# VectorE's tables behind the last pair's low halves, and part of the bias and group 0's projections ahead of the last bias rows

## The chip, the cores and the metric

The kernel runs on one core of a Trainium2 chip. The metric is device microseconds (us) of one execution; lower is better. TensorE (PE in the profile), VectorE (DVE), ScalarE (ACT), GpSimd (POOL) and SyncE (SP, which issues all the DMAs here) have a queue of instructions each, taken in order, and meet only at semaphores.

## The reference

The input `x` has the shape (1, 160, 160, 64). With all the rest left out, what is computed is:

```python
z = ln_c(x)                                          # layer norm over the 64 channels
bias = einsum('bijd,dh->bhij', z, Wb)                # 4 heads, from ALL 160 rows of z
q, k, v = z @ Wq, z @ Wk, z @ Wv                     # per row r: 160 tokens, 4 heads of 32
sim = einsum('brihe,brjhe->brhij', q, k) * scale + bias[:, None]
sim = where(mask, sim, -1e9)
o = softmax(sim) @ v
x = x + (o * sigmoid(z @ Wg)) @ Wo
t = ln_t(x)
probs = softmax(t @ router_w + router_b); top 2 of 8, normed
x = x + sum of the two experts' (t @ expert_w + expert_b), weighted
```

The bias of every attention row is made from all 160 rows of `z`, so nothing after `sim` can start until the layer norm of the whole input is done.

## The kernel before

**Phase 1** runs over 20 pairs of groups (a group is 4 rows of 160 tokens, a pair 8 rows) with `run_phase1`. Of pair n, VectorE makes sums and centres the input, ScalarE squares it, GpSimd scales it, ScalarE takes the float16 high half (`high`, L494) and VectorE the low half (`low`, L680, tile `hl`). TensorE turns it (`turn`, L975), ScalarE copies the turned pair out (`make_xs`, L502, semaphore `xs_made`), TensorE multiplies it by `Wb` (`bias_of`, L987), ScalarE evacuates that (L513, semaphore `b_evac`), and SyncE writes the turned pair to `xs_all` (L239) and the bias rows to a scratch in HBM (L245). The work on one pair is spread over the steps n to n+3. The high and low halves exist because every product is made of float16 pairs.

**Between the phases** VectorE makes tables: `small_tables` (ones and folds), `mask_tables` (the mask as floats, `pen`, `some`, the `pick` matrices), `weight_halves` (high and low halves of all weights, then semaphore `w_ready`), `expert_bias_halves`. All of this is called inside `phase1` at step n == PAIRS (20), which in program order is ahead of the low halves of the last pair, pair 19. Each of these instructions waits for the one before it (`prep`). SyncE reads the bias back in another layout: rows 0 to 127 (the main part) with one DMA into the borrowed tile `pt_a` (L320, semaphore `b_loaded[0]`), and, after the last pair's rows are written, rows 128 to 159 with eight DMAs into `bias_s` and `bias_q` (L326, L328, `b_loaded[1]`). `bias_tables` (VectorE, L758 to L781) and `turn_bias` (TensorE, L1008 to L1014) make of both the tiles `bm` (i along the partitions) and `bt_hi`, `bt_lo` (j along the partitions), with hand-written semaphores `b_step` and `b_turned`; at its end VectorE raises `b_ready`.

**Phase 2** runs over 40 groups with `run_steps`; a step n works on up to seven groups at once. TensorE waits for `w_ready` and, after `turn_bias`, for `b_ready`. Its first work is then `project_qk` of group 0 (L1032, four pieces: q and k, each in two halves of columns), each followed by `qk_high` on ScalarE (L523) and `qk_low` on VectorE (L792); then `max_scores` of group 0 (L1043 adds the bias into `psS`, L1048 and L1053 the products), `row_max` on VectorE (L800), `turn_max`, `scores` (L1068 the bias, L1075 the products) and so on. All orders are written out by hand. A PSUM bank is handed on by `take`, which makes TensorE wait for the last reader of the bank.

Of the kernel before, what the change touches and what calls it, by code (L numbers as in the profile page):

```python
# [5 lines left out]
ALU = mybir.AluOpType  # L6
# [5 lines left out]
P = 128  # L12
# [31 lines left out]
def build(nc, x, Wq, Wk, Wv, Wg, Wo, Wb, router_w, router_b, expert_w, expert_b, mask, out):  # L44
    with ExitStack() as ctx:
# [15 lines left out]
        turned16 = [[banks16[3], banks16[1]], [psS[:, k, :].bitcast(F16) for k in range(2)]]  # L61
        ps_bias = [ps_o, ps_r]

        ident = sb("ident", [P, P])
# [152 lines left out]
        def on(g):  # L217

            return not isinstance(g, int) or 0 <= g < GROUPS

        N_WLOAD = 2 * 6 + 2 + T + 3 * T
# [262 lines left out]
        def _(act):  # L484
# [127 lines left out]
            def step(n, a):  # L612
                b = 1 - a
                if on(n + 1): qk_high(n + 1, b, 0, 1, ps_x)
# [6 lines left out]
                if on(n + 2): qk_high(n + 2, a, 1, 0, ps_m)  # L621
                if on(n + 2): qk_high(n + 2, a, 0, 0, ps_x)
# [8 lines left out]
                if on(n + 2): qk_high(n + 2, a, 1, 1, ps_o)  # L631
# [8 lines left out]
        def _(dve):  # L640
# [54 lines left out]

            def mask_tables():
# [4 lines left out]
                prep(dve.tensor_scalar(pen[:], pen[:], some[:], None, ALU.mult))  # L701
                for c in range(2):
                    prep(dve.tensor_scalar(pick[c][:], pen[:, 0:P], fold[:, 3:4], fold[:, c:c + 1], ALU.mult, ALU.add))
# [11 lines left out]

            def weight_halves():
                prep(dve.tensor_scalar(w_raw[:, Q0:K0], w_raw[:, Q0:K0], SCALE, None, ALU.mult))
                prep(dve.tensor_scalar(w_raw[:, K0:WALL], w_raw[:, K0:WALL], some[:], None, ALU.mult))
                for part in (slice(Q0, WALL), slice(V0, B0), slice(O0, Q0)):
# [14 lines left out]
            def phase1(n, a, do):  # L734
# [18 lines left out]
            def bias_tables():  # L753

                b32 = bias32[:].rearrange("p h s j -> p (h s j)")[:, 0:H * N].rearrange("p (h j) -> p h j", h=H)
                over_heads = lambda v: v.unsqueeze(1).broadcast_to([P, H, N])
                dve.wait_ge(b_loaded[0], 16)
                prep(dve.tensor_tensor(b32, b32, over_heads(mask_f[:]), ALU.mult))  # L758
                prep(dve.tensor_copy(bias_c[:], b32[:, :, P:N]))
                dve.nop().then_inc(b_step, 1)  # L760
                prep(dve.tensor_tensor(bm3[:, :, 0:2, :], b32.unsqueeze(2).broadcast_to([P, H, 2, N]),
                                       pen[:].unsqueeze(1).unsqueeze(1).broadcast_to([P, H, 2, N]), ALU.add))
                dve.wait_ge(b_loaded[1], 16 * 2 * H)
                prep(dve.tensor_tensor(bias_s[:], bias_s[:], mask_f[:], ALU.mult))
                dve.nop().then_inc(b_step, 1)
                prep(dve.transpose(bias_t[:, P:N], bias_s[:, P:N]))
                prep(dve.tensor_tensor(bias_q[:], bias_q[:], over_heads(mask_f[:]), ALU.mult))
                prep(dve.tensor_tensor(bm3[:, :, 2, :], bias_q[:], over_heads(pen[:]), ALU.add))
                dve.wait_ge(b_turned, 2)
                i_rest = ps_o[:, 0:P].rearrange("j (h i) -> j h i", h=H)  # L770
                prep(dve.tensor_copy(bias_t[:, 0:P], ps_r[:, 0:P]))
                prep(dve.tensor_copy(bt3_hi[:, :, 0, 0:P], psS[:, :, 0:P]))
                prep(dve.tensor_copy(bt3_hi[:, :, 0, P:N], i_rest))
                prep(dve.tensor_tensor(bt3_lo[:, :, 0, 0:P], psS[:, :, 0:P], bt3_hi[:, :, 0, 0:P], ALU.subtract))
                prep(dve.tensor_tensor(bt3_lo[:, :, 0, P:N], i_rest, bt3_hi[:, :, 0, P:N], ALU.subtract))
                dve.nop().then_inc(b_step, 1)
                prep(dve.tensor_copy(bt3_hi[:, :, 1, :], bt3_hi[:, :, 0, :]))
                prep(dve.tensor_copy(bt3_lo[:, :, 1, :], bt3_lo[:, :, 0, :]))
                dve.wait_ge(b_turned, 3)
                prep(dve.tensor_copy(bt3_hi[:, :, 2, :], psS[:, :, 0:N]))  # L780
                prep(dve.tensor_tensor(bt3_lo[:, :, 2, :], psS[:, :, 0:N], bt3_hi[:, :, 2, :], ALU.subtract))  # L781
                dve.nop().then_inc(b_ready, 1)

            bias_tables()

            def qk_low(g, a, k, c, bank):

                dve.wait_ge(qkh_done[k][c], g + 1)
                for half_ in range(2):
                    need(dve, sa_done[half_], g - 1)  # L790
                cols = slice(CH * c, CH * c + CH)
                dve.scalar_tensor_tensor(out=qk_lo[a][k][:, cols], in0=bank[:, 0:CH], scalar=1.0 / UP,  # L792
                                         in1=qk_hi[a][k][:, cols], op0=ALU.mult, op1=ALU.subtract).then_inc(qkl_done[k][c], 1)

            def row_max(g, c):
# [131 lines left out]
            def step(n, a):  # L927
# [10 lines left out]
                if on(n - 3): weigh(n - 3, 4, ps_o)  # L938
                if on(n + 2): qk_low(n + 2, a, 1, 0, ps_m)
                if on(n + 2): qk_low(n + 2, a, 0, 0, ps_x)  # L940
                if on(n + 1): row_max(n + 1, 1)
# [8 lines left out]
                for k in range(10, 13):  # L950
                    if on(n - 2): route(n - 2, k)
                if on(n + 2): qk_low(n + 2, a, 1, 1, ps_o)
                for k in range(1, 3):
# [6 lines left out]
                if on(n - 1): mean2(n - 1, b)  # L960
                if on(n + 2): qk_low(n + 2, a, 0, 1, ps_x)
                if on(n + 2): row_max(n + 2, 0)
# [7 lines left out]
        def _(pe):  # L970
# [246 lines left out]
            def step(n, a):  # L1217
# [9 lines left out]
                if on(n - 2): project_out(n - 2, ps_m)  # L1227
                if on(n + 1): project_qk(n + 1, b, 0, 1, ps_x)
                if on(n - 1): project_v_rest(n - 1, b, ps_o)
# [12 lines left out]
                if on(n - 3): experts(n - 3, b, 4, ps_o)  # L1242
                if on(n + 2): project_qk(n + 2, a, 1, 0, ps_m)
                if on(n + 2): project_qk(n + 2, a, 0, 0, ps_x)
                if on(n - 2): turn2(n - 2, a, ps_r, banks16[2])
# [5 lines left out]
                if on(n): row_sums(n, a, ps_m)  # L1251
                if on(n + 2): project_qk(n + 2, a, 1, 1, ps_o)
# [33 lines left out]
```

## Time and profile before

| | us |
|---|---|
| median of 3 runs | 954.86 |
| lowest and highest | 951.77 and 955.25 |
| time of the profiled execution | 954.15 |
| its span, first to last instruction | 952.3 |

The page's own time of 954.15 us and the span of 952.3 us differ by 1.85 us, which lie before the first and behind the last instruction. Phase 1 ends near 98 us in the trace, the stretch between the phases reaches to about 131 us, and phase 2 takes the remaining 820 us. In the rows, "busy" is time in an instruction, "idle before" is the wait ahead of it on its engine, and what stands behind "<-" is the instruction that ended that wait.

### The profile page before, as it was taken

How to read it: one execution, taken by the hardware profiler on the slowest of the kernel's cores; microseconds unless marked ns; L12 is line 12 of the kernel's file. 1: busy time of each engine (PE TensorE's matmuls, PEld its weight loads, DVE VectorE, ACT ScalarE, POOL GpSimd, SP SyncE). 2: the span in 40 equal slices, each digit the busy share in tenths (PEclk: the TensorE clock that was granted, in tenths of full speed). 3: DMA queues.
4: the chain of work that ended last, by engine and by line, in shares of the span. 5: the costliest groups of instructions: out<-in, count | busy, mean ns of one | idle time of the engine just before them, and what ended most of it. 6: DMA issues, size and time to landing. Idle time of an engine off the chain costs nothing.

```text
span 952.3 us, 40372 instructions
## 1 busy us (share of the span) xinstructions
PE 791.2 (83%) x15174; PEld 500.7 (53%) x15174; DVE 767.4 (81%) x1808; ACT 487.8 (51%) x1061; POOL 663.4 (70%) x1092
## 2 busy tenths in 40 slices
PE   1444147999999999999999999999999999999753
PEld 1333123666665666666656665666566656565521
DVE  7776553588889888988898889888888888888764
ACT  3777113465555554655465546554655465546411
POOL 7899000257777767777777777767776777677877
PEclk9999998999999999999999999999999999999965
DMA  3554310000110011001100110011001100100000
GB/s 115 181 194 166 101 39 23 24 23 31 51 38 30 28 48 34 28 28 48 34 28 28 47 36 28 28 48 34 28 28 41 41 28 28 46 32 24 17 13 17
DMA packets 38088, 44.76 MB, mean 47 GB/s; under 512 B 6416, under 2 KB 32656, under 8 KB 38032
## 3 DMA queue, kind: packets, MB, share of 16 engines
q1 hardware_dynamic: 38032, 43.99, 13.9%
q8 instruction: 38, 0.62, 0.3%
q14 instruction: 18, 0.15, 0.0%
HBM read 14.48 MB, written 9.83 MB: 26 GB/s over the span
## 4 chain that ended last, share of the span: by engine, by line
PE 34%; DVE 34%; issue 20%; POOL 8%; ACT 1%; DVEq 1%; DMA 1%; SPq 0%; POOLq 0%; ACTq 0%
DVE negm L800 6%; PE psS L1068 6%; DVE rinv L816 4%; PE psS L1043 4%; POOL ln_s L393 4%; DVE prod L915 3%; PE ps_o L1125 3%; PE ps_x L1125 2%; PE ps_x L1128 2%; PE ps_o L1128 2%; DVE og L831 2%; DVE rt L877 2%; DVE q_lo L792 2%; POOL xn L396 2%; DVE ogu L823 1%
## 5 line engine op out<-in xcount | busy, mean ns | idle before, releaser
L443 POOL TENSOR_TENSOR add<-prod 128x256 f32<-128x256 f32 x160 | 116.3, 727 | 100.7 <-DVE prod L915 100.7
L800 DVE TENSOR_REDUCE negm<-psS 128x12 f16<-128x1920 f32 x80 | 146.0, 1825 | 12.0 <-PE psS L1053 8.2
L494 ACT ACTIVATE hl<-xn 128x320 f16<-128x320 f32 (+1 forms) x60 | 33.5, 559 | 158.3 <-POOL xn L396 156.8
L393 POOL TENSOR_TENSOR ln_s<-ln_v,half 128x5 f32<-128x5 f32 (+1 forms) x60 | 97.0, 1616 | 4.7
L448 POOL TENSOR_TENSOR add<-add 128x128 f32<-128x128 f32 x200 | 91.0, 455 | 0.1
L425 POOL TENSOR_TENSOR rinv_lo<-rinv,rinv_hi 128x160 f16<-128x160 f32 x40 | 19.7, 492 | 100.9 <-ACT rinv_hi L564 100.9
L533 ACT ACTIVATE pt_b<-psS 128x1920 f32<-128x1920 f32 x40 | 70.8, 1771 | 19.6 <-PE psS L1087 15.6
L450 POOL TENSOR_TENSOR ymix<-add 128x64 f32<-128x64 f32 x200 | 64.3, 322 | 15.7
L489 ACT ACTIVATE sq<-xc 128x320 f32<-128x320 f32 (+1 forms) x60 | 33.3, 556 | 81.7 <-POOL xc L409 73.1
L431 POOL TENSOR_TENSOR og_lo<-og,og_hi 128x320 f16<-128x320 f32 x80 | 61.6, 791 | 17.3 <-ACT og_hi L570 17.3
L1043 PE MATMUL psS<-bm,ident 128*128 128x480 f16 (+1 forms) x320 | 68.4, 337 | 5.9 <-ACT pt_a L533 3.3
L1068 PE MATMUL psS<-bt_hi,ident 128*128 128x320 f16 (+1 forms) x320 | 67.9, 335 | 2.3 <-DVE negm L800 2.3
L831 DVE TENSOR_TENSOR og<-ogu,ps_x 128x320 f32<-128x320 f32 x40 | 19.5, 488 | 62.0 <-issue 59.1
L1068 PE MATMUL psS<-bt_lo,ident 128*128 128x320 f16 (+1 forms) x320 | 68.0, 336 | 0.0
L540 ACT ACTIVATE v_main<-ps_x 128x512 f32<-128x512 f32 x40 | 23.9, 597 | 66.3 <-PE ps_x L1139 66.3
L396 POOL TENSOR_TENSOR xn<-xc,ln_s 128x320 f32<-128x320 f32 (+1 forms) x60 | 54.0, 901 | 5.3 <-POOL ln_s L393 1.1
L915 DVE SCALAR_TENSOR_TENSOR prod<-ps_m,coef 128x512 f32<-128x512 f32 x80 | 54.8, 684 | 2.5 <-PE ps_m L1201 2.5
L1191 PE MATMUL ps_m<-w_hi,og_hi 128*128 128x64 f16 x200 | 27.9, 207 | 30.7 <-DVE rinv L816 22.9
L533 ACT ACTIVATE pt_a<-psS 128x1280 f32<-128x1280 f32 x40 | 49.5, 1237 | 2.3 <-PE psS L1077 2.3
L816 DVE RECIPROCAL rinv<-ps_m 128x160 f32<-128x160 f32 x40 | 45.8, 1145 | 1.7 <-PE ps_m L1101 1.7
L1043 PEld LDWEIGHTS psS<-bm,ident 128*128 128x128 f16 x320 | 27.2, 98 | 35.4 <-ACT pt_a L533 16.6
L1191 PEld LDWEIGHTS ps_m<-w_hi,og_hi 128*128 128x128 f16 x200 | 23.9, 128 | 38.0 <-DVE rinv L816 19.2
(263 smaller groups left out, 2819.3 us busy)
## 6 DMA issues: line engine op xcount, KB each, us to landing
xin<-in_x SPq DMA_DIRECT2D x20, 320.0 KB, 2.9
xs_all<-xs_pair SPq DMA_DIRECT2D x20, 320.0 KB, 2.5
xs_q<-xs_all SPq DMA_DIRECT2D x40, 160.0 KB, 2.1
xs_v<-xs_all SPq DMA_DIRECT2D x40, 160.0 KB, 2.1
xin<-in_x SPq DMA_DIRECT2D x40, 160.0 KB, 2.2
out<-res SPq DMA_DIRECT2D x40, 160.0 KB, 1.9
bias_scratch<-b_stage SPq DMA_DIRECT2D x20, 160.0 KB, 2.4
pt_a<-bias_scratch SPq DMA_DIRECT2D x1, 320.0 KB, 3.2
```

The costliest lines, as they stand in the source:

```text
L393: pool.tensor_tensor(ln_s[a][:, 3, 0:w], ln_v[a][:, 0:w], half[:, 0:w], ALU.pow).then_inc(own, 1)
L396: pool.tensor_tensor(xn[a][:, 0:w], xc[a][:, 0:w], ln_s[a][:, 3, 0:w].unsqueeze(2).broadcast_to([P, w, D]), ALU.mult).then_inc(own, 1)
L431: pool.tensor_tensor(og_lo[:, cols], og[:, cols], og_hi[:, cols], ALU.subtract).then_inc(ogl_done[c], 1)
L443: pool.tensor_tensor(add1[t % 2][:], prod_of(t)[:, 0:4, :], prod_of(t)[:, 4:8, :], ALU.add).then_inc(mix_step[t], 1)
L448: pool.tensor_tensor(add2[t % 2][:], add1[t % 2][:, 0:2, :], add1[t % 2][:, 2:4, :], ALU.add).then_inc(mix_step[t], 1)
L450: pool.tensor_tensor(ymix[:, t, :], add2[t % 2][:, 0, :], add2[t % 2][:, 1, :], ALU.add).then_inc(mix_step[t], 1)
L533: act.activation(pt[:].rearrange("p h s i -> p h (s i)"), psS[:, :, 0:slots * N], ACT.Exp).then_inc(exp_done[c], 1)
L800: dve.tensor_reduce(negm[c][:, :, 0:slots], psS[:, :, 0:slots * N].rearrange("i h (s j) -> i h s j", s=slots), AX.X, ALU.max, negate=True) ...
L816: dve.reciprocal(rinv[:], bank[:, 0:N]).then_inc(rinv_done, 1)
L915: dve.scalar_tensor_tensor(out=prod_of(t)[:], in0=bank[:].rearrange("p (e c) -> p e c", e=E), scalar=1.0 / UP, in1=coef[:, t, :].unsqueeze ...
L1043: mm(psS[:, h, 0:(3 - c) * N], lhsT=ident16[:], rhs=bm3[:, h].rearrange("i s j -> i (s j)")[:, 0:(3 - c) * N], start=True, stop=False)
L1068: mm(psS[:, h, 0:slots * N], lhsT=ident16[:], rhs=part[:, h].rearrange("j s i -> j (s i)")[:, 0:slots * N], start=part is bt3_hi, stop=False)
```

## The change

Five edits are made together.

1. The tables are no longer made inside `phase1`. All of phase 1 comes first on VectorE, the low halves of pair 19 among it.
2. The tables are cut in parts: `key_mask` (mask, `pen`, `some`, and the scaling of the q and k weights) and the halves of the output, q and k weights (`slice(Q0, WALL)` is q and k) come first and raise `w_ready` to 1; then come `small_tables` and `mask_tables`.
3. The projections of group 0 are issued ahead of `turn_bias` on TensorE, with their high halves on ScalarE and their low halves on VectorE behind `mask_tables`. They use the banks `ps_x` and `ps_m`, each twice. In the steps, `later(g)` leaves them out for group 0.
4. `bias_tables` is cut in two. `bias_of_keys` does what rows 0 to 127 allow, and the halves of the other weights and of the expert bias come behind it; `w_ready` becomes 2 there. `bias_of_rest` waits for the last rows.
5. The copies of slot 0 into slot 1 of `bt_hi` and `bt_lo` are cut in two: the first 128 columns are copied as before, and the last 32 are made a second time from PSUM.

```diff
@@ phase 1 of VectorE, step n == PAIRS
-                if not do[0]:
-                    if n == PAIRS:
-                        dve.wait_ge(w_loaded, 16 * N_WLOAD)
-                        small_tables()
-                        mask_tables()
-                        weight_halves()
-                        expert_bias_halves()
@@ VectorE, behind run_phase1
-            bias_tables()
+            dve.wait_ge(w_loaded, 16 * N_WLOAD)
+            key_mask()
+            weight_halves([slice(Q0, WALL)])
+            small_tables()
+            mask_tables()
+            for c in range(2):
+                for k in range(2):
+                    qk_low(0, 0, k, c, ahead_bank[k])
+            def bias_of_keys():
...
+                dve.wait_ge(b_loaded[0], 16)
+                prep(dve.tensor_tensor(b32, b32, over_heads(mask_f[:]), ALU.mult))
+                prep(dve.tensor_copy(bias_c[:], b32[:, :, P:N]))
+                dve.nop().then_inc(b_step, 1)
+                prep(dve.tensor_tensor(bm3[:, :, 0:2, :], twice(b32),
+                                       pen[:].unsqueeze(1).unsqueeze(1).broadcast_to([P, H, 2, N]), ALU.add))
+                dve.wait_ge(b_turned, 1)
+                prep(dve.tensor_copy(bias_t[:, 0:P], ps_r[:, 0:P]))
+                prep(dve.tensor_copy(bt3_hi[:, :, 0, 0:P], psS[:, :, 0:P]))
+                prep(dve.tensor_tensor(bt3_lo[:, :, 0, 0:P], psS[:, :, 0:P], bt3_hi[:, :, 0, 0:P], ALU.subtract))
+                prep(dve.tensor_copy(bt3_hi[:, :, 1, 0:P], bt3_hi[:, :, 0, 0:P]))
+                prep(dve.tensor_copy(bt3_lo[:, :, 1, 0:P], bt3_lo[:, :, 0, 0:P]))
+            def bias_of_rest():
...
+                dve.wait_ge(b_loaded[1], 16 * 2 * H)
+                prep(dve.tensor_tensor(bias_s[:], bias_s[:], mask_f[:], ALU.mult))
+                dve.nop().then_inc(b_step, 1)
+                prep(dve.transpose(bias_t[:, P:N], bias_s[:, P:N]))
+                dve.nop().then_inc(b_step, 1)
+                prep(dve.tensor_tensor(bias_q[:], bias_q[:], over_heads(mask_f[:]), ALU.mult))
+                prep(dve.tensor_tensor(bm3[:, :, 2, :], bias_q[:], over_heads(pen[:]), ALU.add))
+                dve.wait_ge(b_turned, 2)
+                i_rest = ps_o[:, 0:P].rearrange("j (h i) -> j h i", h=H)
+                for s in range(2):
+                    prep(dve.tensor_copy(bt3_hi[:, :, s, P:N], i_rest))
+                    prep(dve.tensor_tensor(bt3_lo[:, :, s, P:N], i_rest, bt3_hi[:, :, s, P:N], ALU.subtract))
+                dve.wait_ge(b_turned, 3)
+                prep(dve.tensor_copy(bt3_hi[:, :, 2, :], psS[:, :, 0:N]))
+                prep(dve.tensor_tensor(bt3_lo[:, :, 2, :], psS[:, :, 0:N], bt3_hi[:, :, 2, :], ALU.subtract))
+                dve.nop().then_inc(b_ready, 1)
+            bias_of_keys()
+            weight_halves([slice(V0, B0), slice(O0, Q0)])
+            expert_bias_halves()
+            bias_of_rest()
@@ ScalarE, behind run_phase1
+            for c in range(2):
+                for k in range(2):
+                    qk_high(0, 0, k, c, ahead_bank[k])
@@ TensorE, behind run_phase1
             pe.wait_ge(w_ready, 1)
             pe.wait_ge(xs_made, PAIRS)
+            for c in range(2):
+                for k in range(2):
+                    project_qk(0, 0, k, c, ahead_bank[k])
             pe.wait_ge(b_evac, PAIRS)
             turn_bias()
+            pe.wait_ge(w_ready, 2)
             pe.wait_ge(b_ready, 1)
             run_steps(pe, step)
@@ in every step of TensorE, ScalarE and VectorE (one line shown)
-                if on(n + 2): project_qk(n + 2, a, 1, 0, ps_m)
+                if later(n + 2): project_qk(n + 2, a, 1, 0, ps_m)
```

How the change moves instructions shows at three places. The first is VectorE at the end of phase 1, where `hl` is the tile of the high and low halves. Before, the last tables (the expert bias, `eb_`) stand ahead of the last `hl`, that of pair 19, and the bias follows in one piece:

```order
L730 TENSOR_SCALAR eb_diff<-eb_diff,is_lo 128x320
L731 SCALAR_TENSOR_TENSOR eb_sel<-eb_hi,is_lo,eb_diff 128x320
L680 TENSOR_TENSOR hl<-xn,hl 128x10x64
L758 TENSOR_TENSOR pt_a<-pt_a,mask_f 128x640
L759 COPY bias_c<-pt_a 128x128
L761 TENSOR_TENSOR bm<-pt_a,pen 128x4x320
L764 TENSOR_TENSOR bias_s<-bias_s,mask_f 128x160
L766 STREAM_TRANSPOSE bias_t<-bias_s 128x32
```

In the changed kernel the same place on VectorE reads as follows; the first `hl` of the two is that of pair 18, the second that of pair 19:

```order
L685 TENSOR_REDUCE ln_s<-sq 128x10
L689 TENSOR_TENSOR hl<-xn,hl 128x10x64 x2
L707 CAST mask_f<-mask_u 128x160
L708 TENSOR_REDUCE some<-mask_f 128x1
L709 TENSOR_SCALAR pen<-mask_f 128x160
L710 TENSOR_SCALAR pen<-pen,some 128x160
L711 TENSOR_SCALAR w_raw<-w_raw 128x128
L712 TENSOR_SCALAR w_raw<-w_raw,some 128x128
L731 TENSOR_SCALAR w_hi<-w_raw 128x256
L732 SCALAR_TENSOR_TENSOR w_lo<-w_raw,w_hi 128x256
L693 MEMSET quad 32x1
```

The low halves of pair 19 have moved ahead of every table, and the halves of the q and k weights ahead of the small tables. The second place is VectorE behind `mask_tables` in the changed kernel, where `q_lo` and `k_lo` are the low halves of group 0:

```order
L762 SCALAR_TENSOR_TENSOR q_lo<-ps_x,q_hi 128x320
L762 SCALAR_TENSOR_TENSOR k_lo<-ps_m,k_hi 128x320
L762 SCALAR_TENSOR_TENSOR q_lo<-ps_x,q_hi 128x320
L762 SCALAR_TENSOR_TENSOR k_lo<-ps_m,k_hi 128x320
L780 TENSOR_TENSOR pt_a<-pt_a,mask_f 128x640
L781 COPY bias_c<-pt_a 128x128
L783 TENSOR_TENSOR bm<-pt_a,pen 128x4x320
L786 COPY bias_t<-ps_r 128x128
L787 CAST bt_hi<-psS 128x4x128
L788 TENSOR_TENSOR bt_lo<-psS,bt_hi 128x4x128
L789 COPY bt_hi<-bt_hi 128x4x128
L790 COPY bt_lo<-bt_lo 128x4x128
```

Group 0's low halves have moved from behind the whole bias to ahead of it. The third place is TensorE between the phases. Before, it turns the bias (`pt_a`, `bias_c`, `bias_s`, `bias_t`), projects group 0 and then adds the bias of the maxima (`bm`):

```order
L1008 MATMUL psS<-ident,pt_a 128x128 x4
L1009 MATMUL ps_r<-ident,bias_c 128x128
L1011 MATMUL ps_o<-ident,bias_s 128x128
L1014 MATMUL psS<-bias_t,spread 128x160 x4
L1032 MATMUL ps_m<-xs_q,w_hi 128x320
L1033 MATMUL ps_m<-xs_q,w_lo 128x320
L1032 MATMUL ps_x<-xs_q,w_hi 128x320
L1033 MATMUL ps_x<-xs_q,w_lo 128x320
L1032 MATMUL ps_o<-xs_q,w_hi 128x320
L1033 MATMUL ps_o<-xs_q,w_lo 128x320
L1032 MATMUL ps_x<-xs_q,w_hi 128x320
L1033 MATMUL ps_x<-xs_q,w_lo 128x320
```

In the changed kernel TensorE's queue there is:

```order
L1055 MATMUL ps_x<-xs_q,w_lo 128x320
L1054 MATMUL ps_m<-xs_q,w_hi 128x320
L1055 MATMUL ps_m<-xs_q,w_lo 128x320
L1030 MATMUL psS<-ident,pt_a 128x128 x4
L1031 MATMUL ps_r<-ident,bias_c 128x128
L1033 MATMUL ps_o<-ident,bias_s 128x128
L1036 MATMUL psS<-bias_t,spread 128x160 x4
L1065 MATMUL psS<-bm,ident 128x480 x4
L1070 MATMUL psS<-k_hi,q_hi 128x160 x8
```

All eight matmuls of group 0's projections have moved ahead of the turns of the bias, and `max_scores` of group 0 (`psS<-bm,ident`) follows those turns at once.

## Rows read from the trace of the kernel before

**Rows 1.** The page's first part: busy time of each engine, share of the span.

```profile
PE 791.2 (83%) x15174; PEld 500.7 (53%) x15174; DVE 767.4 (81%) x1808; ACT 487.8 (51%) x1061; POOL 663.4 (70%) x1092
```

**Rows 2.** Chain that ended last, in order of time: start us, us, what.

```profile
106.79 1.24 PE psS L975 x10
...
111.00 3.96 DMA bias_scratch<-b_stage
...
118.21 2.02 DMA bias_q<-bias_scratch
```

**Rows 3.** Timeline of DVE: start us, us, line, operation, [idle before <-releaser].

```profile
92.92 0.06 DVE L684 MEMSET quad<- 32x1 f32 x1
...
96.08 0.24 DVE L698 CAST mask_f<-mask_u 128x160 f32<-128x160 uint8 x1
...
97.33 0.35 DVE L703 TENSOR_SCALAR pick<-pen,fold 128x128 f16<-128x128 f32 x1
...
100.12 0.23 DVE L717 TENSOR_SCALAR w_raw<-w_raw 128x128 f32<-128x128 f32 x1
...
101.49 0.56 DVE L720 TENSOR_SCALAR w_hi<-w_raw 128x776 f16<-128x776 f32 x1
...
103.71 0.18 DVE L726 TENSOR_SCALAR rb<-rb 128x40 f32<-128x40 f32 x1 [0.16 <-DVE w_lo L721]
...
105.82 0.82 DVE L680 TENSOR_TENSOR hl<-xn,hl 128x640 f16<-128x640 f32 x1
106.56 0.82 DVE L758 TENSOR_TENSOR pt_a<-pt_a,mask_f 128x640 f32<-128x640 f32 x1
...
107.80 1.49 DVE L761 TENSOR_TENSOR bm<-pt_a,pen 128x1280 f16<-128x1280 f32 x1 [0.16 <-DVE bias_c L759]
120.32 0.32 DVE L764 TENSOR_TENSOR bias_s<-bias_s,mask_f 128x160 f32<-128x160 f32 x1 [11.03 <-DMA bias_q<-bias_scratch]
...
121.05 0.82 DVE L767 TENSOR_TENSOR bias_q<-bias_q,mask_f 128x640 f32<-128x640 f32 x1
...
122.77 0.29 DVE L771 COPY bias_t<-ps_r 128x128 f32<-128x128 f32 x1
123.09 0.69 DVE L772 CAST bt_hi<-psS 128x512 f16<-128x512 f32 x1
...
125.31 0.33 DVE L777 COPY bt_hi<-bt_hi 128x640 f16<-128x640 f16 x1 [0.15 <-DVE bt_lo L775]
...
126.33 0.82 DVE L780 CAST bt_hi<-psS 128x640 f16<-128x640 f32 x1 [0.32 <-PE psS L1014]
...
131.65 0.49 DVE L792 SCALAR_TENSOR_TENSOR q_lo<-ps_x,q_hi 128x320 f16<-128x320 f32 x1 [0.75 <-ACT q_hi L523]
```

**Rows 4.** Timeline of ACT at the last pair's high halves, same columns.

```profile
94.91 0.74 ACT L494 ACTIVATE hl<-xn 128x640 f16<-128x640 f32 x1
```

**Rows 5.** Timeline of PE, same columns.

```profile
97.69 0.38 PE L988 MATMUL ps_o<-xs_pair,wb 128*32 128x160 f16 x4
...
112.10 0.42 PE L1009 MATMUL ps_r<-ident,bias_c 128*128 128x128 f32 x1
...
128.12 0.45 PE L1032 MATMUL ps_m<-xs_q,w_hi 128*128 128x320 f16 x1 [1.93 <-DVEq L782]
...
130.43 0.45 PE L1032 MATMUL ps_x<-xs_q,w_hi 128*128 128x320 f16 x1 [0.52 <-DVE q_lo L792]
...
131.72 1.76 PE L1043 MATMUL psS<-bm,ident 128*128 128x480 f16 x4 [0.57 <-issue]
```

**Rows 6.** Chain that ended last, later: bias matmuls of three steps.

```profile
149.51 3.38 PE psS L1068 x8
...
168.93 1.79 PE psS L1068 x8
...
186.15 1.76 PE psS L1068 x8
```

**Rows 7.** Busy time in 2 us; PEclk is TensorE's granted clock.

```profile
148.00:150.00 2.00, 0.49 (x2) 0.25 (x3) 1.63 (x2) 0.00 (x0) 0.00 (x0) 0.50 0.00 0
```

More of the change, by code:

```diff
@@ L62, in build @@
         ps_bias = [ps_o, ps_r]
+        ahead_bank = [ps_x, ps_m]
         ident = sb("ident", [P, P])
@@ L219, in on, with later @@
             return not isinstance(g, int) or 0 <= g < GROUPS
+        def later(g):
+            return on(g) and not (isinstance(g, int) and g == 0)
         N_WLOAD = 2 * 6 + 2 + T + 3 * T
@@ L613, in step @@
                 b = 1 - a
-                if on(n + 1): qk_high(n + 1, b, 0, 1, ps_x)
+                if later(n + 1): qk_high(n + 1, b, 0, 1, ps_x)
                 if on(n - 1): keep_v_rest(n - 1, b, ps_o)
@@ L620, in step @@
                 if on(n + 1): tanh_gate(n + 1, b, 0, ps_r)
-                if on(n + 2): qk_high(n + 2, a, 1, 0, ps_m)
-                if on(n + 2): qk_high(n + 2, a, 0, 0, ps_x)
+                if later(n + 2): qk_high(n + 2, a, 1, 0, ps_m)
+                if later(n + 2): qk_high(n + 2, a, 0, 0, ps_x)
                 if on(n - 2): keep_xs2(n - 2, a, banks16[2])
@@ L630, in step @@
                 if on(n + 1): keep_m(n + 1, b, 1, ps_r)
-                if on(n + 2): qk_high(n + 2, a, 1, 1, ps_o)
+                if later(n + 2): qk_high(n + 2, a, 1, 1, ps_o)
                 if on(n): rinv_high(n)
@@ L694, in small_tables, with key_mask @@
                 prep(dve.tensor_copy(spread[:], fold[:].unsqueeze(1).broadcast_to([P, RG, DH])))
-            def mask_tables():
+            def key_mask():
                 prep(dve.tensor_copy(mask_f[:], mask_u8[:]))
@@ L701, in mask_tables @@
                 prep(dve.tensor_scalar(pen[:], pen[:], some[:], None, ALU.mult))
+                prep(dve.tensor_scalar(w_raw[:, Q0:K0], w_raw[:, Q0:K0], SCALE, None, ALU.mult))
+                prep(dve.tensor_scalar(w_raw[:, K0:WALL], w_raw[:, K0:WALL], some[:], None, ALU.mult))
+            def mask_tables():
                 for c in range(2):
@@ L714, in mask_tables, with weight_halves @@
                         prep(dve.tensor_copy(pick_rest[c][:], pick_f[:]))
[L716 to L719, printed above, removed]
+            def weight_halves(parts):
+                for part in parts:
                     prep(dve.tensor_scalar(w_hi[:, part], w_raw[:, part], UP, None, ALU.mult))
@@ L741, in phase1 @@
                 if do[2]: low(n - 2, a, T2, hi_ready, lo_ready)
-                if not do[0]:
-                    if n == PAIRS:
-                        dve.wait_ge(w_loaded, 16 * N_WLOAD)
-                        small_tables()
-                        mask_tables()
-                        weight_halves()
-                        expert_bias_halves()
-            run_phase1(dve, phase1)
[L753 to L782, printed above, removed]
@@ L793, in qk_low @@
                                          in1=qk_hi[a][k][:, cols], op0=ALU.mult, op1=ALU.subtract).then_inc(qkl_done[k][c], 1)
+            dve.wait_ge(w_loaded, 16 * N_WLOAD)
[7 more added lines that the diff above has]
+            def bias_of_keys():
+                b32 = bias32[:].rearrange("p h s j -> p (h s j)")[:, 0:H * N].rearrange("p (h j) -> p h j", h=H)
+                over_heads = lambda v: v.unsqueeze(1).broadcast_to([P, H, N])
+                twice = lambda v: v.unsqueeze(2).broadcast_to([P, H, 2, v.shape[-1]])
+                dve.wait_ge(b_loaded[0], 16)
[10 more added lines that the diff above has]
+                prep(dve.tensor_copy(bt3_lo[:, :, 1, 0:P], bt3_lo[:, :, 0, 0:P]))
@@ new lines, in bias_of_rest @@
+            def bias_of_rest():
+                over_heads = lambda v: v.unsqueeze(1).broadcast_to([P, H, N])
+                dve.wait_ge(b_loaded[1], 16 * 2 * H)
[14 more added lines that the diff above has]
+                dve.nop().then_inc(b_ready, 1)
@@ L938, in step @@
                 if on(n - 3): weigh(n - 3, 4, ps_o)
-                if on(n + 2): qk_low(n + 2, a, 1, 0, ps_m)
-                if on(n + 2): qk_low(n + 2, a, 0, 0, ps_x)
+                if later(n + 2): qk_low(n + 2, a, 1, 0, ps_m)
+                if later(n + 2): qk_low(n + 2, a, 0, 0, ps_x)
                 if on(n + 1): row_max(n + 1, 1)
@@ L951, in step @@
                     if on(n - 2): route(n - 2, k)
-                if on(n + 2): qk_low(n + 2, a, 1, 1, ps_o)
+                if later(n + 2): qk_low(n + 2, a, 1, 1, ps_o)
                 for k in range(1, 3):
@@ L960, in step @@
                 if on(n - 1): mean2(n - 1, b)
-                if on(n + 2): qk_low(n + 2, a, 0, 1, ps_x)
+                if later(n + 2): qk_low(n + 2, a, 0, 1, ps_x)
                 if on(n + 2): row_max(n + 2, 0)
@@ L1227, in step @@
                 if on(n - 2): project_out(n - 2, ps_m)
-                if on(n + 1): project_qk(n + 1, b, 0, 1, ps_x)
+                if later(n + 1): project_qk(n + 1, b, 0, 1, ps_x)
                 if on(n - 1): project_v_rest(n - 1, b, ps_o)
@@ L1242, in step @@
                 if on(n - 3): experts(n - 3, b, 4, ps_o)
-                if on(n + 2): project_qk(n + 2, a, 1, 0, ps_m)
-                if on(n + 2): project_qk(n + 2, a, 0, 0, ps_x)
+                if later(n + 2): project_qk(n + 2, a, 1, 0, ps_m)
+                if later(n + 2): project_qk(n + 2, a, 0, 0, ps_x)
                 if on(n - 2): turn2(n - 2, a, ps_r, banks16[2])
@@ L1251, in step @@
                 if on(n): row_sums(n, a, ps_m)
-                if on(n + 2): project_qk(n + 2, a, 1, 1, ps_o)
+                if later(n + 2): project_qk(n + 2, a, 1, 1, ps_o)
                 if on(n): project_v(n, a, ps_x)
```

## The prediction

> **What bounds the kernel now.** I first read the busy shares on the page. TensorE is busy 83% of the span and VectorE 81% [rows 1], so in phase 2 these two bind each other, and the change leaves phase 2's work as it is. What can move is the stretch between the phases, so next I read the chain that ended last from 90 to 132 us and beside it each engine's timeline. There the chain has one thread. VectorE works through its tables from 92.92 to 105.82 us, and only then makes the low halves of pair 19 [rows 3], whose high halves ScalarE had ready at 94.91 + 0.74 = 95.65 us [rows 4]. TensorE turns the pair at 106.79 us, the last bias rows are written from 111.00 us, and the reads of rows 128 to 159 end at 118.21 + 2.02 = 120.23 us [rows 2]. VectorE stands idle for 11.03 us before it can use them [rows 3]. It then works until TensorE may start group 0 at 128.12 us, and the first score work of phase 2 starts at 131.72 us [rows 5]. So two things cost time: 12.9 us of tables ahead of a 0.8 us instruction on which all else hangs, and 11.0 us of idle VectorE behind it. They are one loss seen twice, and must not be added.
>
> **The low halves of pair 19.** They start at about 95.68 us instead of 105.82 us; before that VectorE waits for ScalarE some 2.8 us (the tables that covered this are behind it now). TensorE does not follow by the full 10.1 us. Its queue has the bias products of pair 18 in front, which end at 97.69 + 0.38 = 98.07 us [rows 5], so the turn starts at 98.15 us instead of 106.79 us: 8.6 us earlier. From there to the landing of the last reads nothing changes but the start, since turn, copy, product, write and read follow each other with no VectorE in them: 120.23 - 8.6 = 111.6 us.
>
> **VectorE's own work is the new bound.** I add up its new order with the differences between starts in rows 3, which hold the waits between dependent instructions.
> - Low halves: 106.56 - 105.82 = 0.74, from 95.68 to 96.42.
> - `key_mask` is 97.33 - 96.08 = 1.25; the scaling and the q and k halves are 101.49 - 100.12 = 1.37. `w_ready` is 1 at 99.04.
> - `small_tables` is 96.08 - 92.92 = 3.16; the `pick` tables are 100.12 - 97.33 = 2.79. They end at 104.99.
> - Group 0's low halves. TensorE has the last pair's bias products in front, which end before their write at 111.00 - 8.6 = 102.4 us [rows 2], and the first two projections and high halves are done before 104.99. The first q low half takes 0.49. The second q piece must wait for its bank: from TensorE's start at 130.43 to the low half at 131.65 is 1.22 us of round trip [rows 3, 5]. So 0.49 + 0.05 + 1.22 takes it to 106.75, and two more low halves of about 0.53 to 107.8.
> - `bias_of_keys`: 107.80 - 106.56 = 1.24 and then 1.53 for `bm`, to 110.57. TensorE's turns are released near 109.0; before, released by the end of the bias copy, they ended at 112.10 + 0.42 = 112.5 us, 1.5 us behind the last bias rows' evacuation at 111.0 [rows 2, 5]. They end near 110.5 and are hidden under `bm`. Then one copy of 123.09 - 122.77 = 0.32, two operations on 512 columns of 0.69 with their gaps (0.73), and two copies inside SBUF of 512 columns at about 0.31: 2.4, to 112.97.
> - The other weights: 103.71 - 101.49 = 2.22; the expert bias: 105.82 - 103.71 = 2.11. Both to 117.30.
> - `bias_of_rest`: the rows landed at 111.6, 5.7 us ago, so there is no wait. 121.05 - 120.32 = 0.73 and 122.77 - 121.05 = 1.72; four operations on 128 columns of `ps_o`, as wide as that of 122.77 us, at 0.32 = 1.28; the two last of 0.82 with their gaps, 1.72. That is 5.45, to 122.75. TensorE's two turns of the rest lie under the `bias_q` work.
>
> `b_ready` thus comes at 122.75 us instead of 128.05: 5.3 us earlier, not 8.6, because VectorE has run out of idle time and 2.8 us of it went ahead of the low halves.
>
> **The projections of group 0.** Behind `b_ready` TensorE used to need 131.72 - 128.12 = 3.6 us for the four projections and their round trip [rows 5]. They are gone from there, as the high and low halves lie before. Their VectorE share of 2.8 us is in the sum above. The first score work starts at 122.80 us instead of 131.72: **8.9 us earlier**. The other edits (two copies from PSUM in place of part of two copies of 0.33 us) are in the sum; `w_ready` at 2 is long raised when TensorE asks. SyncE has no wait moved: reads of group 0's second tiles and of the v columns stand behind the bias reads and move with them. If SyncE were late for one, its cover would be several us of scores.
>
> **Does it reach the end?** From 131.72 us on each engine has the same order and waits only for the others, so the whole of phase 2 shifts. The sum is 954.15 - 8.9 = 945.3 us against the profiled execution. That execution lies 0.7 us under the median of 954.86, against which the sum is 946.0. I take 945.8 us.
>
> **TensorE's clock.** The first score work ran at the lower of the two clock levels: the four bias matmuls took 1.76 us, 0.44 each [rows 5]. In 148 to 150 us the granted clock is 0.50, the 1.2 GHz level [rows 7], and the eight bias matmuls that start there took 3.38 us, 0.42 each, against 1.79 and 1.76 us, 0.22 each, in the next two steps. The step that begins with them lasted 168.93 - 149.51 = 19.4 us and the next 186.15 - 168.93 = 17.2 us [rows 6]: such a dip costs some 2.2 us.
>
> The Trainium skill, in "TensorE: Matmul & The Clock Gate", section "HAM oscillation — how this bites in real kernels", says that waits between bursts of matmuls drop the clock and that each new burst starts at half rate. The dip in this trace agrees with it (0.50 behind sparse matmuls), and it speaks against the change, which takes TensorE's projections away from directly ahead of the first scores.
>
> **The rivals.**
> - *A, the shift holds* (above): 945.8 us, by itself 942.5 to 949. Chance 0.80.
> - *B, only one half of it counts.* If the last pair's path did not come forward (another wait ahead of the turn, or VectorE's longer list eating the gain), only the projections' 3.6 us would be left: 951.2 us. Against it: the turn's other inputs are ready at 98.07 [rows 5]. For it: VectorE has no slack in the whole stretch, so 3 us more of waits in the twenty-odd dependent steps would show at the end. Chance 0.09.
> - *C, the clock.* Colder matmuls at the start of phase 2. One more dip or a rise one burst later costs 2.2 us and gives 948.0, inside A's range. It turns the change to slower only when it costs over 8.9 us, which is four such dips more, that is, TensorE near 1.2 GHz through most of the first two score steps. That would give 956 to 960 us. For it: sparse matmuls from 98 to 122 us; against it: the trace before was as sparse there, and the scores themselves come at the same spacing. Chance 0.03.
> - *D, it gains more.* If the dip of 148 us does not come in the new alignment, 2.2 us fall away, and if the clock rises ahead of 128 us another 1 to 2: 942 to 943.6. Chance 0.08.
>
> **How the numbers follow.** A measurement of this kernel tells about 0.5%, 4.8 us, from no change; faster by more means under 950.1 us. A and D lie there, and a small part of B; the rest of B is within 0.5%. The shares are faster 0.89, same 0.08, slower 0.03. The range takes A and D, with the run-to-run spread of 3.5 us shifted by 8.9: from 951.77 - 8.9 = 942.9 down to 942.0 for D, and from 955.25 - 8.9 + 2.2 = 948.6 up to 950.0 for a few waits of 0.3 us that the sum misses.
>
> **What would show it.** In the profile of the changed kernel: the low halves of pair 19 near 95.7 us and the turn near 98.2; the bias reads landed near 111.6; VectorE without an idle stretch above 1 us from 96 to 122 us, and `bias_s` near 117.3 without a wait for a DMA; the first `psS<-bm` matmul near 122.8. A wait of VectorE for a DMA ahead of `bias_s` would say that I have placed the landing wrong. Same first scores but a later end would say that phase 2 gave it back, by the clock if the granted clock is 0.50 in longer stretches than before.

## The result, and the profile after

| | before | changed |
|---|---|---|
| median, us | 953.69 | 946.38 |
| lowest to highest, us (4 runs each) | 951.77 to 955.25 | 945.64 to 947.85 |
| profiled execution, us (span) | 954.15 (952.3) | 946.58 (944.4) |

The ratio is 0.9918 with a 95% interval of 0.9893 to 0.9942: the change gains 7.3 us between the medians, 7.6 us between the profiled executions. Forecast were 945.8 us and a gain of 8.9 us. (The median of before is of four runs here; the 954.86 us of the prediction was of three.)

VectorE's timeline of the changed kernel between the phases (start us, us, line and operation, in brackets the idle time ahead and its releaser):

```profile
95.96 0.83 DVE L689 TENSOR_TENSOR hl<-xn,hl 128x640 f16<-128x640 f32 x1 [2.71 <-ACT hl L499]
96.70 0.24 DVE L707 CAST mask_f<-mask_u 128x160 f32<-128x160 uint8 x1
...
105.38 0.49 DVE L762 SCALAR_TENSOR_TENSOR q_lo<-ps_x,q_hi 128x320 f16<-128x320 f32 x1
...
107.15 0.49 DVE L762 SCALAR_TENSOR_TENSOR q_lo<-ps_x,q_hi 128x320 f16<-128x320 f32 x1 [0.88 <-ACT q_hi L528]
...
109.32 1.49 DVE L783 TENSOR_TENSOR bm<-pt_a,pen 128x1280 f16<-128x1280 f32 x1 [0.16 <-DVE bias_c L781]
...
113.28 0.57 DVE L731 TENSOR_SCALAR w_hi<-w_raw 128x776 f16<-128x776 f32 x1
...
117.61 0.32 DVE L796 TENSOR_TENSOR bias_s<-bias_s,mask_f 128x160 f32<-128x160 f32 x1
...
122.34 0.82 DVE L809 TENSOR_TENSOR bt_lo<-psS,bt_hi 128x640 f16<-128x640 f32 x1
125.86 2.16 DVE L822 TENSOR_REDUCE negm<-psS 128x12 f16<-128x1920 f32 x1 [2.70 <-PE psS L1075]
```

The low halves of pair 19 stand at 95.96 instead of 105.82 us, and the wait of 11.03 us ahead of `bias_s` [rows 3] is gone: that row has no brackets now. From 96 to 123.16 us (122.34 + 0.82) the longest wait is 0.88 us, for the second round of group 0. VectorE's list is the bound there.

TensorE's timeline of the same execution:

```profile
98.29 1.25 PE L997 MATMUL psS<-ident,hl 128*128 128x128 f16 x10
...
105.92 0.45 PE L1054 MATMUL ps_x<-xs_q,w_hi 128*128 128x320 f16 x1 [2.74 <-DVE q_lo L762]
...
109.37 1.09 PE L1030 MATMUL psS<-ident,pt_a 128*128 128x128 f32 x4 [2.20 <-DVEq L782]
...
118.05 0.48 PE L1033 MATMUL ps_o<-ident,bias_s 128*128 128x128 f32 x1 [7.38 <-DVEq L797]
...
123.32 1.76 PE L1065 MATMUL psS<-bm,ident 128*128 128x480 f16 x4 [3.95 <-issue]
...
133.64 1.22 PE L1090 MATMUL psS<-bt_hi,ident 128*128 128x320 f16 x4
134.66 1.27 PE L1090 MATMUL psS<-bt_lo,ident 128*128 128x320 f16 x4
...
138.94 0.97 PE L1065 MATMUL psS<-bm,ident 128*128 128x480 f16 x4 [1.45 <-ACT pt_a L542]
```

The turn of pair 19 starts at 98.29 instead of 106.79 us [rows 2], and the first scores at 123.32 instead of 131.72 us [rows 5]: 8.4 us earlier. Their four matmuls take the same 1.76 us. Of SyncE's queue:

```profile
101.69 1.20 SPq L250 DMA_DIRECT2D bias_scratch<-b_stage  x2
104.71 1.75 SPq L331 DMA_DIRECT2D bias_s<-bias_scratch  x4
106.50 1.82 SPq L333 DMA_DIRECT2D bias_q<-bias_scratch  x4
```

The last of these reads is issued at 107.9 us, and the reads of `bias_q` take 2.0 to 2.2 us from there to their landing (2.02 us before [rows 2]). So the last rows are there at about 110.0 us, 7.6 us before VectorE comes to them. (Counted from the end of the issuing instruction it would be 110.3 us, the figure that two of the expectations below use.) The chain that ended last carries the shift on. Its rows of the changed kernel that answer to those of 168.93 and 186.15 us before [rows 6] are:

```profile
161.13 1.79 PE psS L1090 x8
...
178.32 1.79 PE psS L1090 x8
```

That is 7.8 us earlier both times, and the spans differ by 952.3 - 944.4 = 7.9 us: what is gained by the third score step arrives at the end.

### The profile page after: what moved, and what is told of

Read it like the earlier page. It is cut to its first block, busy times and chain, and to the rows that moved or that the text cites. A ratio compares the mean times of both kernels' runs of the same rounds, so it can differ in the third digit from the quotient of the medians.

```text
span 944.4 us, 40376 instructions
## 1 busy us (share of the span) xinstructions
PE 791.5 (84%) x15174; PEld 500.7 (53%) x15174; DVE 767.1 (81%) x1810; ACT 488.1 (52%) x1061; POOL 664.0 (70%) x1092
## 4 chain that ended last, share of the span: by engine, by line
DVE 34%; PE 34%; issue 20%; POOL 9%; ACT 1%; DVEq 1%; DMA 0%; POOLq 0%; SPq 0%; ACTq 0%
DVE negm L822 6%; PE psS L1090 6%; PE psS L1065 4%; DVE rinv L838 4%; POOL ln_s L398 4%; DVE prod L937 3%; PE ps_o L1147 3%; PE ps_x L1150 2%; PE ps_x L1147 2%; PE ps_o L1150 2%; DVE og L853 2%; DVE rt L899 2%; DVE q_lo L762 2%; POOL xn L401 2%; DVE ogu L845 2%
```

## The experiments

"First scores" below is the start of the first `psS<-bm` matmul in that kernel's profile, "step 3" the start of the eight bias matmuls that stand at 186.15 us before. The four kernels from "tables alone" to "deferred" shared a chip and seven runs of before (median 955.23 us), the three below them another chip and thirteen runs (954.08 us), and the ratio is to the runs of before of the same set. The change itself has a set of its own (953.69 us), so medians of different sets are compared with some care.

| kernel | median, us | ratio to before (95%) | first scores | step 3 |
|---|---|---|---|---|
| before | | | 131.72 | 186.15 |
| changed | 946.38 | 0.9918 (0.9893 to 0.9942) | 123.32 | 178.32 |
| tables alone | 945.80 | 0.9897 (0.9880 to 0.9913) | 123.93 | 178.85 |
| projections alone | 950.54 | 0.9940 (0.9921 to 0.9959) | 128.57 | 184.64 |
| not projected ahead | 946.22 | 0.9910 (0.9894 to 0.9927) | 123.61 | 177.23 |
| deferred | 941.78 | 0.9859 (0.9841 to 0.9877) | 118.97 | 174.00 |
| extra matmuls | 946.07 | 0.9908 (0.9882 to 0.9933) | 123.58 | 177.48 |
| deferred more | 939.64 | 0.9837 (0.9772 to 0.9902) | 117.11 | 173.21 |
| both | 940.12 | 0.9838 (0.9772 to 0.9903) | 116.32 | 172.14 |

### The tables alone

The kernel before, with the block of tables moved as it stands:

```diff
-                if not do[0]:
-                    if n == PAIRS:
-                        dve.wait_ge(w_loaded, 16 * N_WLOAD)
-                        small_tables()
-                        mask_tables()
-                        weight_halves()
-                        expert_bias_halves()
             run_phase1(dve, phase1)
+            dve.wait_ge(w_loaded, 16 * N_WLOAD)
+            small_tables()
+            mask_tables()
+            weight_halves()
+            expert_bias_halves()
```

> Edit 1 alone: all tables move as one block behind phase 1 on VectorE; the bias stays in one piece and group 0 is projected behind it, as before. Theory (VectorE's list between the phases becomes the bound, whatever its inner order): the low halves of pair 19 start near 95.7 us, and with no idle time left VectorE needs 128.05 - 92.92 - 11.03 = 24.1 us from there, so b_ready comes near 119.8 and the first scores near 123.4 us, 8.3 us earlier than before and within 0.2 us of the changed kernel; time about 946 us. Rival (the cut of the tables and the projections ahead are what brings it, 3.6 us of it from the projections alone): first scores near 127 us, time about 950.

VectorE's timeline of this kernel:

```profile
96.09 0.83 DVE L680 TENSOR_TENSOR hl<-xn,hl 128x640 f16<-128x640 f32 x1 [2.71 <-ACT hl L494]
...
112.54 0.33 DVE L761 TENSOR_TENSOR bias_s<-bias_s,mask_f 128x160 f32<-128x160 f32 x1
```

And TensorE's:

```profile
123.93 1.76 PE L1040 MATMUL psS<-bm,ident 128*128 128x480 f16 x4 [0.57 <-issue]
```

The first scores come at 123.93 us (7.8 us of gain, forecast 8.3; 0.4 us of the difference is the later end of phase 1, low halves at 96.09 instead of 95.7), 0.6 us behind the changed kernel, and the two cannot be told apart in time (945.80 against 946.38 us, in different sets). `bias_s` has no wait for a DMA here either. The idle 11 us are gone by this edit alone. The rival is refuted.

### The projections alone

The kernel before, with edit 3 and `qk_low` of group 0 ahead of the whole of `bias_tables`:

```diff
+            for c in range(2):
+                for k in range(2):
+                    qk_low(0, 0, k, c, ahead_bank[k])
             bias_tables()
@@ TensorE
+            for c in range(2):
+                for k in range(2):
+                    project_qk(0, 0, k, c, ahead_bank[k])
             pe.wait_ge(b_evac, PAIRS)
             turn_bias()
```

> Edit 3 alone: group 0 is projected ahead of the bias turns, with its high and low halves, but the tables stay ahead of the low halves of pair 19. Theory: the last bias rows still land near 120.2 us and b_ready stays near 128.05, the projections lie in VectorE's idle 11 us, so first scores at 128.1 instead of 131.72 us: 3.6 us gained, time about 950. The two single edits then add up to some 12 us where the whole change has 8.4, because with the tables moved the projections cost VectorE 2.8 us of its list. Rival (gains add): e1 plus e2 equals the whole.

VectorE's timeline of this kernel:

```profile
106.19 0.82 DVE L689 TENSOR_TENSOR hl<-xn,hl 128x640 f16<-128x640 f32 x1
...
112.01 0.49 DVE L799 SCALAR_TENSOR_TENSOR q_lo<-ps_x,q_hi 128x320 f16<-128x320 f32 x1 [4.99 <-ACT q_hi L528]
...
120.77 0.33 DVE L773 TENSOR_TENSOR bias_s<-bias_s,mask_f 128x160 f32<-128x160 f32 x1 [3.32 <-DMA bias_q<-bias_scratch]
```

The work ahead eats into the idle time (3.32 us are left of 11.03), and `bias_s` still starts at 120.8 us. The first scores are at 128.57 instead of 131.72 us, 3.2 us of gain; with the low halves 0.37 us later than before in this execution (106.19 against 105.82), that is 3.5 of the 3.6 us expected. So the single edits bring 7.8 + 3.2 = 11.0 us, against 8.4 for the whole. They do not add.

### Not projected ahead

The changed kernel with `later` back to `on` for group 0, and the three loops ahead taken out:

```diff
-            for c in range(2):
-                for k in range(2):
-                    project_qk(0, 0, k, c, ahead_bank[k])
@@ in every step (one line shown)
-                if later(n + 2): project_qk(n + 2, a, 1, 0, ps_m)
+                if on(n + 2): project_qk(n + 2, a, 1, 0, ps_m)
```

> The changed kernel with group 0 projected behind the bias again (edit 3 undone, the others kept). Theory: VectorE's list is 2.7 us shorter, b_ready near 120.5, then 3.6 us of projections, first scores near 124.1: 0.8 us later than in the changed kernel, time about 947. Rival (the projections' 3.6 us count in full): first scores near 127, time 950.

```profile
123.61 1.76 PE L1059 MATMUL psS<-bm,ident 128*128 128x480 f16 x4 [0.57 <-issue]
```

On TensorE's timeline the first scores are 0.3 us later than in the changed kernel. The low halves of pair 19 were 0.58 us earlier in this execution (95.38 against 95.96), so counted from there the cost is 0.9 us, with 0.8 expected. The second profiles of both kernels give 0.9 us again (first scores 28.24 and 27.36 us behind the low halves). By the medians the two are the same. Within the whole change, the projections ahead are worth under 1 us: they remove 3.6 us behind `b_ready` and put 2.7 us into VectorE's list ahead of it.

### Deferred

The changed kernel, with two blocks taken out of the list ahead of `b_ready`. TensorE asks for `w_ready` at 2 only behind `max_scores` of group 0:

```diff
@@ VectorE, behind bias_of_keys()
-            weight_halves([slice(V0, B0), slice(O0, Q0)])
-            expert_bias_halves()
             bias_of_rest()
+            weight_halves([slice(V0, B0), slice(O0, Q0)])
@@ VectorE's step
+                if isinstance(n, int) and n == -1: expert_bias_halves()
                 if later(n + 2): qk_low(n + 2, a, 0, 1, ps_x)
@@ TensorE's step
                 if on(n + 1): max_scores(n + 1, b, 0)
+                if isinstance(n, int) and n == -1: pe.wait_ge(w_ready, 2)
@@ TensorE, behind turn_bias()
-            pe.wait_ge(w_ready, 2)
             pe.wait_ge(b_ready, 1)
```

> The changed kernel with 4.3 us of VectorE's list taken out from ahead of b_ready: the halves of the other weights stand behind b_ready, where VectorE waited 2.7 us for the first scores, and the expert bias halves stand in a wait of 3.9 us in the step that starts phase 2. Theory (VectorE's list is the bound; the last rows have landed near 110.3, 7 us before they are used): b_ready and the first scores 4.3 us earlier, near 119.0, time about 942. Rival (the DMA of the last rows or TensorE's turns bind): less than 1 us gained.

VectorE's timeline of this kernel:

```profile
113.30 0.33 DVE L796 TENSOR_TENSOR bias_s<-bias_s,mask_f 128x160 f32<-128x160 f32 x1
...
121.54 2.16 DVE L821 TENSOR_REDUCE negm<-psS 128x12 f16<-128x1920 f32 x1 [0.47 <-PE psS L1075]
```

The first scores are at 118.97 us, 4.35 us earlier, for 4.33 us of work taken out; step 3 is 4.3 us earlier and the median 4.6 us lower (against the runs of before of each set, some 13 us are gained instead of 7.3). The 4.33 us of VectorE's list ahead of `b_ready` counted in full. The weights' halves cost nothing in their new place: the wait ahead of the first `negm` is 0.47 instead of 2.70 us.

### Extra matmuls

The changed kernel, with 13 matmuls between the bias turns and `b_ready`, whose results nobody reads:

```diff
             turn_bias()
+            pe.wait_ge(xq_loaded[1], 16)
+            pe.wait_ge(qkl_done[1][1], 1)
+            for _ in range(13):
+                mm(ps_m[:, 0:CH], lhsT=w_hi[:, Q0:Q0 + P], rhs=xs_q[1][:, 0:CH], start=True, stop=True)
```

> The changed kernel with 13 extra matmuls of 320 columns on TensorE behind the bias turns, where it waited from 119.4 to 123.3 us for b_ready; their results are overwritten unread. Clock theory (the first scores run at the lower of the two clock levels because TensorE had been idle): the four bias matmuls take about 1.0 us instead of 1.76, the stretch to the first exponent (137.16 us) shrinks by 1 to 4 us, time about 943 to 945. Rival (the length of these matmuls has another cause, such as operands or the bank): 1.76 us stays and so does the time, 946.4.

TensorE's timeline of this kernel:

```profile
119.56 3.48 PE L1288 MATMUL ps_m<-xs_q,w_hi 128*128 128x320 f16 x13
123.58 0.97 PE L1065 MATMUL psS<-bm,ident 128*128 128x480 f16 x4 [0.53 <-issue]
...
132.87 1.23 PE L1090 MATMUL psS<-bt_hi,ident 128*128 128x320 f16 x4
133.89 1.27 PE L1090 MATMUL psS<-bt_lo,ident 128*128 128x320 f16 x4
```

Its busy time in stretches of 2 us, with the granted clock third from the end:

```profile
126.00:128.00 2.00, 0.35 (x3) 0.27 (x4) 1.47 (x2) 0.02 (x1) 0.00 (x0) 0.54 0.00 0
128.00:130.00 2.00, 2.00 (x9) 1.16 (x8) 0.49 (x1) 1.58 (x4) 0.00 (x0) 0.50 0.00 0
```

The first part came as the clock theory has it: the same four matmuls take 0.97 instead of 1.76 us. But while VectorE takes its maxima TensorE is idle for 2.63 us, the granted clock falls (0.54 in 126 to 128 us, 0.50 behind that), and the next matmuls are as slow as without the extra ones. Step 3 is 0.8 us earlier than in the first profile of the changed kernel and no earlier than in its second (177.39 us), and the median of 946.07 us does not differ from 946.38; the 943 to 945 us expected did not come. The clock is the cause of the 1.76 us, and these 13 matmuls did not hold it over the wait that follows.

### Deferred more, and both

Beside the two blocks of "deferred", the `pick` matrices are made in the waits of the first score step, part 0 behind `rest_max` and part 1 behind `row_max(0, 1)`; TensorE waits for them (`w_ready` at 3) inside `scores`:

```diff
             small_tables()
-            mask_tables()
@@ VectorE's step
                 if on(n + 1): rest_max(n + 1)
+                if isinstance(n, int) and n == -1: mask_tables((0,))
...
                 if on(n + 1): row_max(n + 1, 1)
+                if isinstance(n, int) and n == -1:
+                    mask_tables((1,))
+                    dve.nop().then_inc(w_ready, 1)
```

> As the kernel that defers the other weights and the expert bias, and besides the pick matrices (2.8 us) stand in VectorE's waits of the first score step. Theory: group 0's first low half now waits for ScalarE near 103.2 us instead of the tables near 105.4, so only 2.2 of the 2.8 us count: first scores 4.3 + 2.2 = 6.5 us earlier than in the changed kernel, near 116.8, time about 940. If VectorE's list were the only bound, 7.1 us; if the bias reads (landed near 110.3) bind, less than 6.

VectorE's timeline of this kernel:

```profile
102.77 0.49 DVE L762 SCALAR_TENSOR_TENSOR q_lo<-ps_x,q_hi 128x320 f16<-128x320 f32 x1 [0.67 <-ACT q_hi L528]
...
111.44 0.32 DVE L795 TENSOR_TENSOR bias_s<-bias_s,mask_f 128x160 f32<-128x160 f32 x1 [0.81 <-DMA bias_q<-bias_scratch]
```

Two other waits now appear in VectorE's list: 0.67 us for ScalarE's high halves, as expected, and 0.81 us for the bias reads. The chain that ended last has the last of them at 107.43 + 3.92 = 111.35 us, where such a read took 2.0 to 2.2 us in the changed kernel; why this one took longer was not tried. The first scores are at 117.11 us, 6.2 us ahead of the changed kernel (6.5 expected), but phase 1 ended 0.46 us earlier here (low halves at 95.50 instead of 95.96 us). Counted from there it is 5.8 us, under the 6 us that the expectation set for the case in which the bias reads bind. This is the fastest median, 939.64 us, though its interval (0.9772 to 0.9902) holds the whole of that of "deferred". The last kernel joins it with the 13 extra matmuls.

> The further deferral together with the 13 extra matmuls. Theory: the two are independent, since one shortens VectorE's list and the other the matmuls behind b_ready; the sum of the two single gains, time 936 to 940. Rival: the faster scores run into the deferred tables and gain nothing more.

Its VectorE timeline shows the rival:

```profile
118.58 2.16 DVE L820 TENSOR_REDUCE negm<-psS 128x12 f16<-128x1920 f32 x1 [0.16 <-DVE w_lo L732]
```

The first maxima wait for `w_lo`, the deferred weights, and no longer for TensorE. The first scores are 0.79 us earlier than in "deferred more", which is the DMA wait of 0.81 us that this execution did not have; counted from the low halves (95.49 us) they are 6.5 us ahead of the changed kernel, the full gain that "deferred more" was expected to bring. Step 3 is 1.1 us earlier than in "deferred more", but in time nothing is gained that the medians show (940.12 against 939.64 us, with 936 to 940 expected).

### Second profiles, for the clock

In the first profile of the changed kernel the eight matmuls of the first bias of scores, at 133.64 us, took 2.3 us. In the first profile of before they took 1.25 us:

```profile
142.00 0.70 PE L1068 MATMUL psS<-bt_hi,ident 128*128 128x320 f16 x4
142.54 0.71 PE L1068 MATMUL psS<-bt_lo,ident 128*128 128x320 f16 x4
...
145.74 0.97 PE L1043 MATMUL psS<-bm,ident 128*128 128x480 f16 x4 [1.45 <-ACT pt_a L533]
```

Four kernels were each profiled once more.

> A second look at the kernel before, for TensorE's clock alone. If projections directly ahead of the first scores bring the clock up sooner (theory from four looks), the eight matmuls that add the first bias of scores take about 1.25 us again, as in the first look. If it is a matter of chance between executions, 1.25 or 2.3.

> A second look at the changed kernel. If the missing projections let the clock rise later, the same eight matmuls take about 2.3 us again; if it is chance, 1.25 or 2.3.

> A second look at the changed kernel with group 0 projected behind the bias. Theory of the projections: 1.25 us as in its first look. Chance: 1.25 or 2.3.

> A second look at the kernel with only the tables moved, which also projects group 0 directly ahead of the first scores but showed 2.2 us in its first look. Theory of the projections: that look was the exception, 1.25 us now. Chance: 1.25 or 2.3.

TensorE's timeline of the changed kernel, second profile:

```profile
122.83 1.76 PE L1065 MATMUL psS<-bm,ident 128*128 128x480 f16 x4 [3.95 <-issue]
...
133.12 0.70 PE L1090 MATMUL psS<-bt_hi,ident 128*128 128x320 f16 x4
133.66 0.71 PE L1090 MATMUL psS<-bt_lo,ident 128*128 128x320 f16 x4
```

All four took 1.25 us, the changed kernel and the one with only the tables moved among them, which had shown 2.3 and 2.2. So the moment at which the clock rises differs between executions of one kernel. That does not make it pure chance. Of the six profiles of kernels that project group 0 directly ahead of the first scores (before, "tables alone" and "not projected ahead", two each), five show 1.25 us and one 2.2. Of the five of kernels that project it ahead of the bias and have no extra matmuls (changed twice, "projections alone", "deferred", "deferred more"), four show 2.2 to 2.3 us and one 1.25. The missing projections may make the later rise more frequent; these profiles lean that way and are too few to settle it.

In the second profiles before and changed have the same lengths of matmuls up to there, and first scores at 131.85 and 122.83 us: 9.0 us apart. Step 3 stands at 186.42 and 177.39 us, 9.0 us apart too.

The second profiles also price the smaller edits. Counted from the low halves of pair 19, step 3 comes 82.4 and 81.9 us later in the two profiles of the changed kernel, 82.8 and 81.6 us with the tables alone, 81.9 and 82.0 us with group 0 projected behind the bias. What edits 2 to 5 bring at the first scores (0.5 us over the tables alone) is by the third step less than the spread between two executions of one kernel.

## Why the prediction was right

- **The low halves and the last pair's path.** Forecast: low halves near 95.7, turn near 98.15 us. Measured: 95.96 and 98.29. Phase 1 itself ended 0.28 us later in this execution (ScalarE's high halves at 95.19 instead of 94.91); the differences were right to 0.15 us.
- **The landing of the last rows** was placed at 111.6 and came at about 110.0 us. I had taken the write of the last bias rows over at 3.96 us [rows 2]. SyncE's wait for it was 3.6 us before and 1.8 us in the changed kernel. It changed nothing, since VectorE came 7.6 us later still. The term was wrong, and that it did not matter is the slack's doing.
- **VectorE's list.** Forecast for `b_ready`: 122.75 us; measured 123.16. Of the 0.4 us, 0.28 is the later end of phase 1. "Deferred" confirms that this list is the bound, at a price of 1 to 1.
- **The first scores.** Forecast 8.9 us earlier, measured 8.4 in the first profile and 9.0 in the second; 0.5 us of the difference is where phase 1 ended in the changed kernel (95.96 and 95.47 us for the low halves), 0.1 us is before's own.
- **Does it reach the end?** Yes, less what the clock took. In the first profile the shift falls from 8.4 us at the first scores to 6.8 us (138.94 against 145.74 us for the next `psS<-bm`), because the clock rose one group of matmuls later, and comes back to 7.8 us, since the dip behind it was shorter: the eight matmuls there took 2.24 instead of 3.38 us. This is rival C's mechanism inside A's range, at 1.6 us there and 0.6 us by step 3 where C had 2.2; in the second profiles the shift stays 9.0 us. The forecast gain of 8.9 us and the 7.3 us by the medians differ by 1.6 us, but the runs of one kernel spread over 2 us, so more than that is not shown.
- **The time itself** came within 0.6 us of the forecast (946.38 against 945.8) although the gain was 1.6 us smaller. That closeness is in part luck: the forecast stood on before's median of 954.86 us, and the median measured beside the changed kernel was 1.2 us lower.
- **Rival B** (only 3.6 us count) is refuted: the tables alone bring 7.8 us at the first scores. What I did not see is how little the rest brings. The forecast's sum holds it (the projections take 3.6 us from behind `b_ready` and put 2.8 us into VectorE's list ahead of it), but the text sets out 5.3 and 3.6 us as the two parts of the gain, and "not projected ahead" prices the projections at 0.9 us.
- **The rule on the clock** that the Trainium skill gives ("TensorE: Matmul & The Clock Gate", "HAM oscillation — how this bites in real kernels") agrees in its mechanism with the extra matmuls: 0.97 us behind a busy stretch, 0.50 granted behind a wait of 2.63 us. As a case against the change it weighed little: the first scores ran at the lower level before and after (1.76 us both times), and the rise behind them came late in one profile of the changed kernel and early in the other, with 0.6 us lost by step 3 in the one and nothing in the other.

## What to carry to other kernels

Look in each engine's hand-written order for work that nobody waits for, standing ahead of a short instruction from which a chain over other engines and a DMA round trip starts; move that instruction first, and the idle time behind the round trip takes the tables up. The gain ends where the idle time does: after that the engine's own list is the bound, further reordering inside it brings little, and the next step is to take out of it, into waits that stand behind the handover, what the next stage does not need yet (4.3 us of work for 4.35 us of time here). Two edits that fill the same idle time do not add: 7.8 and 3.2 us alone, 8.4 together.

## What was not expected of the hardware

SyncE waited 3.6 us for the write of the last bias rows in both profiles of before, in "projections alone" and in "extra matmuls", and 1.7 to 1.8 us in the nine other profiles, both of the changed kernel among them. Before, in both profiles, and in "projections alone" the DMA engines moved 0 GB/s from 102 to 110 us, until just ahead of this write, and where the wait was short that gap is missing. But it is missing in "extra matmuls" too (257 GB/s in 102 to 104 us, 77 in 104 to 106), whose edit leaves everything up to this write as in the changed kernel:

```profile
101.95 1.20 SPq L250 DMA_DIRECT2D bias_scratch<-b_stage  x2
106.84 1.75 SPq L331 DMA_DIRECT2D bias_s<-bias_scratch  x4
```

In the changed kernel these two rows stand at 101.69 and 104.71 us. So the quiet ahead of the write does not explain the longer wait by itself, and its cause is open.

The granted clock reads 1.00 from 128 to 140 us before, while the matmuls there run at half the later rate (0.44 us each for 480 columns against 0.22 in the later steps). In the kernel with the extra matmuls, which had the clock up first, the record reads 0.50 for matmuls of the same length. In such a stretch the length of the matmuls tells the level and the record alone does not.
